# Graph layer on one core: TensorE reads the stored edge messages at register addresses, and VectorE's copies of them go

## The reference

```python
msg = jnp.concatenate([x[row], edge_attr], axis=1)      # row = src, col = dst (sorted)
msg = msg @ W1 + b1                                     # 96 -> 128
agg = jax.ops.segment_sum(msg, col, num_segments=x.shape[0])
out = jnp.concatenate([x, agg], axis=1) @ W2 + b2       # 64 + 128 -> 64
y = layernorm(x + out, axis=-1)
```

## Time and profile before

| | |
|---|---|
| median of three runs | 1054.15 us (1051.51 to 1056.91) |
| profiled execution: first to last instruction (span) | 801.0 us |
| the rest of the median, outside that span | 253.15 us |
| TensorE matmuls busy, share of the span | 615.5 us, 77% |
| TensorE weight loads busy | 544.4 us, 68% |
| VectorE busy | 522.7 us, 65% |
| ScalarE busy | 398.6 us, 50% |
| POOL busy | 423.9 us, 53% |
| mean granted TensorE clock | 0.843 of full speed |

### The profile page before, as it was taken

How to read it: one execution, slowest core, us unless ns; L and a number is a source line. 1 busy time by engine, 2 the same in 40 slices (tenths; PEclk the granted TensorE clock), 3 DMA queues, 4 the chain that set the end, 5 groups by cost and what they waited for, 6 DMA issues and landing times. The chain is left out here.

```text
span 801.0 us, 29016 instructions
## 1 busy us (share of the span) xinstructions
PE 615.5 (77%) x8418; PEld 544.4 (68%) x8419; DVE 522.7 (65%) x1826; ACT 398.6 (50%) x2012; POOL 423.9 (53%) x514
## 2 busy tenths in 40 slices
PE   1345445677778888888898898989898888878785
PEld 1344435566767777777777787878777777768675
DVE  3670111354465648858887788788787787878876
ACT  0011122102234344444567777777777777757655
POOL 5676766711676766475467777767466445200000
PEclk9655555657688779979999999999999999989988
DMA  2121222200223233333345545555455455533432
GB/s 63 28 37 36 37 37 34 57 9 12 61 54 82 59 86 79 79 78 79 100 110 139 127 122 139 129 136 147 115 139 144 110 132 134 134 86 115 126 97 81
DMA packets 168753, 71.47 MB, mean 89 GB/s; under 512 B 61570, under 2 KB 162447, under 8 KB 168720
## 3 DMA queue, kind: packets, MB, share of 16 engines
q1 hardware_dynamic: 104592, 51.74, 22.7%
q0 software_dynamic: 12544, 12.87, 8.5%
q10 hardware_dynamic: 51584, 6.41, 5.1%
HBM read 45.37 MB, written 25.60 MB: 89 GB/s over the span
## 5 line engine op out<-in xcount | busy, mean ns | idle before, releaser
L363 POOL DMA_INDIRECT feat<-in_x,src_now x392 | 393.6, 1004 | 255.4 <-issue 94.6
L775 DVE TENSOR_SCALAR onehot<-node_of_col,group_base,dst_of 128x256 bf16<-128x256 bf16 x952 | 287.4, 348 | 106.1 <-issue 78.9
L473 PEld LDWEIGHTS ps_y<-z_window,onehot 128*128 128x128 bf16 x5712 | 202.6, 101 | 65.8 <-DVE z_window L778 46.0
L473 PE MATMUL ps_y<-z_window,onehot 128*128 128x64 bf16 x5712 | 226.7, 198 | 26.6 <-DVE z_window L778 23.5
L574 ACT ACTIVATE square<-ps_y 128x64 bf16<-128x64 f32 x784 | 162.7, 239 | 135.8 <-PE ps_y L464 133.2
L574 ACT ACTIVATION_READ_ACCUMULATOR square<-ps_y 128x1 f32 x784 | 159.5, 224 | 0.0
L539 ACT ACTIVATE feat_t<-ps_t 97x512 f32<-97x512 f32 x98 | 58.6, 598 | 179.8 <-PE ps_z L400 159.9
L400 PE MATMUL ps_z<-wz,feat_t 97*128 97x64 f32 x784 | 123.1, 324 | 24.6 <-DVE z_rest L700 24.5
L400 PEld LDWEIGHTS ps_z<-wz,feat_t 97*128 97x128 f32 x784 | 118.0, 238 | 33.2 <-DVE z_rest L700 31.8
L392 PE MATMUL ps_t<-ident,feat 128*97 128x128 f32 x392 | 72.3, 333 | 86.8 <-DMA feat<-in_x,src_now 63.7
L464 PE MATMUL ps_y<-wx,x_t 128*128 128x128 f32 x784 | 118.4, 296 | 13.1 <-issue 8.7
(11 more groups left out here) (107 smaller groups left out, 226.2 us busy)
## 6 DMA issues: line engine op xcount, KB each, us to landing
xin<-in_x SPq DMA_DIRECT2D x97, 256.0 KB
out<-yout SPq DMA_DIRECT2D x97, 256.0 KB
feat<-in_x,src_now POOLq DMA_INDIRECT x392
feat<-in_edge_attr ACTq DMA_DIRECT2D x97, 64.0 KB
z<-in_src SPq DMA_DIRECT2D x1, 192.0 KB
z<-in_dst SPq DMA_DIRECT2D x1, 192.0 KB
xin<-in_x SPq DMA_DIRECT2D x1, 128.0 KB
out<-yout SPq DMA_DIRECT2D x1, 128.0 KB
```

Of the source, the lines that this page charges most:

```text
L363: nc.gpsimd.indirect_dma_start(out=feat[h][:, half * CB + c, 0:C], out_offset=None, in_=x[:, :], in_offset=bass.IndirectOffsetOnAxis(ap=sr ...
L473: mm = nc.tensor.matmul(ps_y[h][:, col:col + C], onehot[h][:, g, s, a, :], z_window[h][:, g, s, part * C:(part + 1) * C], start=False, sto ...
L775: ins = nc.vector.tensor_scalar(onehot[h][:, g, s, :, :], node_of_col[:, :, :], base, dst_of[:, bass.ds(firsts[g] + (at + s), 1)], ALU.add ...
```

## The change

VectorE's copy into `z_window` is dropped, with the buffers and the two semaphores that told TensorE of it. `pair_sum` takes its moving operand from `z` itself, at chunk `firsts[g] + at + s`, which is only known in a register. So TensorE reads six numbers of a block's table row (the four firsts as well) before the block, no longer two. Since nothing on VectorE now stands between the last part of `z` and TensorE's reading, TensorE waits for `z_kept` ahead of the units of a round. Two index tables of the set-up that lay in `z_window` get tiles of their own (`chunk_order`). Line numbers after line 120 shift by a few.

```diff
-        z_window = [sb(f"z_window{h}", [P, G, 2, 3 * C], bf16) for h in range(2)]
+        chunk_order = [sb(f"chunk_order{h}", [P, CHUNKS]) for h in range(2)]
...
-                _, (second, third) = load_steps(mybir.EngineType.PE, b, G, 2, G * CHUNKS // 2)
+                _, (*firsts, second, third) = load_steps(mybir.EngineType.PE, b, 0, G + 2, G * CHUNKS // 2)
...
-                def pair_sum(g):
+                def pair_sum(g, at):
...
                                 mm = nc.tensor.matmul(ps_y[h][:, col:col + C], onehot[h][:, g, s, a, :],
-                                                      z_window[h][:, g, s, part * C:(part + 1) * C], start=False, stop=False)
+                                                      z[:, firsts[g] + (at + s), part, :], start=False, stop=False)
...
                 for g in range(G):
-                    pe.wait_ge(window_ready, G * b + g + 1)
                     pe.wait_ge(hot_ready, G * b + g + 1)
-                    pair_sum(g).then_inc(group_summed, 1)
+                    pair_sum(g, 0).then_inc(group_summed, 1)
...
-                        pe.wait_ge(window2_ready, turn_no)
                         pe.wait_ge(hot2_ready, turn_no)
-                        pair_sum(g)
+                        pair_sum(g, 2)
                     with pe.If(third > 0):
-                        _, firsts = load_steps(mybir.EngineType.PE, b, 0, G, CHUNKS - 4)
...
                 edge_round(k)
-                for_units(pe, mybir.EngineType.PE, k - LAG, unit)
+                units_of_round = read_units(mybir.EngineType.PE, k - LAG)
+                pe.wait_ge(z_kept, k - LAG)
+                run_units(pe, *units_of_round, unit)
...
                     ins.then_inc(hot, 1)
-                    nc.vector.tensor_copy(z_window[h][:, g, :, :],
-                                          z[:, bass.ds(firsts[g] + at, 2), :, :].rearrange("p s q c -> p s (q c)")
-                                          ).then_inc(window, 1)
```

More of the change, by code:

```diff
@@ L134, in gnn_residual_layernorm @@
         below, holds = (buf[:, 0:CHUNKS] for buf in x_t)
-        chunk_up, chunk_down = (
-            buf[:, :, :, :].rearrange("p g s q -> p (g s q)").bitcast(f32)[:, 0:CHUNKS] for buf in z_window)
+        chunk_up, chunk_down = (buf[:, :] for buf in chunk_order)
         score, least_row, most_row = (
@@ L179, in gnn_residual_layernorm @@
         hot_ready = sem("onehot_ready")
-        window_ready = sem("z_window_ready")
         group_summed = sem("group_summed")
         hot2_ready = sem("onehot_of_second_pair_ready")
-        window2_ready = sem("z_window_of_second_pair_ready")
         hotx_ready = sem2("onehot_x_ready")
@@ L456, in block_sum @@
                 b = 2 * k + h
-                _, (second, third) = load_steps(mybir.EngineType.PE, b, G, 2, G * CHUNKS // 2)
+                _, (*firsts, second, third) = load_steps(mybir.EngineType.PE, b, 0, G + 2, G * CHUNKS // 2)
+                firsts = [nc.s_assert_within(f, 0, CHUNKS - 4, skip_runtime_bounds_check_because="so the table is made")
+                          for f in firsts]
                 pe.wait_ge(y_kept[h], k + 1)
@@ L525, in _ @@
                 edge_round(k)
-                for_units(pe, mybir.EngineType.PE, k - LAG, unit)
+                units_of_round = read_units(mybir.EngineType.PE, k - LAG)
+                pe.wait_ge(z_kept, k - LAG)
+                run_units(pe, *units_of_round, unit)
             edge_round(PAIRS - 1, loads=2)
+            pe.wait_ge(z_kept, PAIRS - 1 - LAG)
             for_units(pe, mybir.EngineType.PE, PAIRS - 1 - LAG, unit)
@@ L770, in one_hots, with pair @@
                 dve.wait_ge(hots_used[h], k + 1)
-                def pair(g, at, hot, window):
+                def pair(g, at, hot):
                     base = group_base[:, bass.ds(b * G + g, 1)]
@@ L777, in pair @@
                     ins.then_inc(hot, 1)
-                    nc.vector.tensor_copy(z_window[h][:, g, :, :],
-                                          z[:, bass.ds(firsts[g] + at, 2), :, :].rearrange("p s q c -> p s (q c)")
-                                          ).then_inc(window, 1)
                 for g in range(G):
-                    pair(g, 0, hot_ready, window_ready)
+                    pair(g, 0, hot_ready)
                 with dve.If(second > 0):
@@ L786, in one_hots @@
                         dve.wait_ge(group_summed, G * b + g + 1)
-                        pair(g, 2, hot2_ready, window2_ready)
+                        pair(g, 2, hot2_ready)
                     with dve.If(third > 0):
```

## The result

The changed kernel takes 1247.01 us (median of 1244.18, 1247.01 and 1249.96 us) against 1054.15 us: 1.1808 times as long, 95% interval 1.1746 to 1.187, or +193 us. The forecast was 1213 us, +159 us, in a range of 1125 to 1300. The direction and the range held. The gain that it counted on did not come, and part of that miss was cancelled by another.

A forecast was written before the change was run, and what follows sets the result against it. VectorE's loop was taken to set the round, with TensorE close behind. On 1054 us: registers +200, seams +38, table +30, `z_kept` +2, ended waits -101, edge transfers -10, in sum +159, gave 1213 us, range 1125 to 1300.

The forecast's parts named there:

- The register instructions, +200 and +38 us: TensorE's pair sums: twelve register-addressed loads take 0.83 us, not 0.41, +200 us over 476 sums; the seams add +38 us.
- the seams: Between TensorE's pair sums: the next turn's add and first register instruction, 0.08 us x 476 = +38 us.
- The table, +30 us: TensorE's table read before each of 98 blocks: six numbers instead of two, 0 to 60 us, half taken, +30 us.
- The wait for `z_kept`, +2 us: TensorE's new wait ahead of a round's units: already met when reached, one register instruction in 49 rounds, +2 us.
- What goes away, -101 and -10 us: TensorE's waits for copies, `z_rest`, `x_t` and two "issue" gaps end, -101 us; edge transfers come early enough, -10 us.
- the register work hides: Rival: TensorE's register instructions fall beside matmuls, so VectorE's gain comes through, 1002 us; chance 0.04.
- The time outside the span, taken as fixed: The 253.15 us between the profiled span of 801.0 us and the 1054.15 us median, assumed unaffected by the change.
- The clock: Rival: gaps between the sums' matmuls lower TensorE's granted clock, 1268 to 1323, say 1295 us; chance 0.13.
- The condition set: Forecast wrong if rounds lengthen while the granted clock in dense stretches is near 0.75; then the clock is the cause.
- The signs: Profile after: six register instructions per twelve loads over 0.8 to 0.9 us, no line 778, VectorE waiting, rounds 13.5 to 15 us.

The follow-up runs named there:

- without hold-ups: Runs without POOL's indirect gathers, where TensorE's matmuls are not held up: changed kernel 997.17 us, kernel before 764.62 us, fixed chunks 771.36 us.
- The run with idle ones: Fixed chunks and no gathers, plus six register instructions per pair sum that count in a register no matmul uses: 956.15 us, ratio 0.9246.
- fixed chunks: The changed kernel, with pair sums reading z at fixed addresses and no register instructions between their matmuls: 1066.82 us, ratio 1.0104.
- the kernel with the longer read: The kernel before, with TensorE reading six numbers of a block's table row instead of two and using the same two: 1077.97 us, ratio 1.0198.

## Why the prediction was right, and where it was not

**The register instructions, +200 and +38 us: right in kind and in cause, and near in size in the condition they were read from.** 0.42 + 0.08 = 0.50 us a pair sum were forecast; without hold-ups 0.47 were measured (226 us). Of these the sums themselves hold 401.5 - 212.4 = 189 us, 0.40 a pair sum; most of the rest is fp32 work that took longer at a lower clock (160.6 against 122.3 us at the dense products). So the 0.08 us for the seams do not show, the clock takes their place, and that 0.47 comes so close to 0.50 is partly luck. In the timed condition it was 0.38 (180 us): in the first blocks of the rounds the hold-up hides the register work, and in the blocks behind them the lower clock hides part of it. Line 504 of the kernel before was the right place to look.

The prediction had the next load wait for its register instruction. The run with idle ones narrows that: they lengthen four pair sums from 1.56 to 3.02 us, both at full clock, though no load depends on them. The Trainium skill, "TensorE: Matmul & The Clock Gate", section "Architectural detail: the array is 16× 32×32, not 1× 128×128", says that TensorE's queue has 64 entries and that weight loads can be pulled ahead of matmuls in flight. By the same two blocks that does not hide register instructions here.

**The table, +30 us:** 21 us alone (TensorE's reads of six have a median of 1.0 us, not the 1.16 taken from VectorE). **The wait for `z_kept`, +2 us:** no wait of TensorE for the parts of `z` appears in the changed kernel's list.

**What goes away, -101 and -10 us: this is the step that failed.** It said that with VectorE ahead TensorE's waits end and its own sequencer is late next. The missing copies give 10 us in the timed condition, and 0 to 11 us without hold-ups. Two reasons, both shown. In the timed condition VectorE does not set the round, since TensorE is held up about 8 us of it; the waits that the forecast counted were hardly there to be saved. The kernel with gathers of consecutive rows, which has the time and the reads of the kernel before, shows 11.8 us of matmul idle time for the copies, 3.1 for `z_rest` and 5.9 for `x_t`. Without hold-ups the waits moved to the table read and to `x_t`, which lay behind them. Besides, the forecast added up waits of weight loads, 46.0 and 31.8 us; in the same trace the matmuls stood idle only 23.5 us for the copies and 24.5 for `z_rest`, and the rest of those waits passed beside matmuls that were still running. The rival "the register work hides", at 1002 us, rested on the same gain and would have failed by it too.

**The time outside the span, taken as fixed: wrong.** There is none beyond 2 us in any run that has both numbers. The 253 us are hold-ups beside the gathers: the span without gathers is 764.0 us, and with the 39 us that the gathers add ahead of the first unit that makes 803, near the profiled 801. That the hold-ups cost both kernels amounts not far apart (252 and 211 us) made the carrying over from 801 to 1054 us harmless, by luck and not by argument.

**The sum:** 159 - 58 (registers 180 and not 238) - 9 (table) - 2 (`z_kept`) + 101 (copies and transfers 10 and not 111) = +191 us; measured +193. A total within 34 us hides two misses of 58 and 101.

**The clock.** The rival had it as a cause of its own. It is a part of the registers' 180 us: the fp32 groups and the bias matmuls are busy about 37 us longer than with fixed chunks (26 at the dense products, 4 at the bias, 3.5 and 3.1 at the transposes). The condition set, that a clock near 0.75 would make the clock the cause, was badly chosen: 0.72 was granted, but 0.77 with fixed chunks, where the loss is gone.

**The signs.** Six register instructions, 0.82 us a pair sum, no line 778, VectorE waiting several microseconds a round: as told. The doubled busy time of the sums (436.8 against 226.7 us) is a weaker sign than it looks, since 62 us of it stand in the kernel with fixed chunks too (288.9). Rounds of 13.5 to 15 us: only without gathers (15.16); in the timed kernel a median of 21.1, against 19.6 with fixed addresses.

## What to carry to other kernels

A register instruction between small matmuls costs TensorE's stream its own time and more (0.046 us by itself, 189 / 2856 = 0.07 us in the sums and 226 / 2856 = 0.08 us with the clock's share here, beside 1.37 / 48 = 0.03 us for such a matmul), so price a register address by the number of such instructions and let an idle engine copy to a fixed place instead. Before the waits of one engine are booked as a gain, ask what stands behind each of them, by a run with the expensive part taken out. And when a profile's span is far below the timed median, the profile is of another condition: find that first, since here the timed runs held 253 us that the profile did not show, more than the change.

## What the runs showed that was not expected

Indirect gathers that POOL issues freely (one every 1.25 us) slow TensorE's stream to one or two matmuls per 0.75 us for 8 to 9 us a round; the same bytes as plain DMAs do not (765 against 1055 us), and with at most two gathers in flight little of it is left (898 us). With one in flight POOL waited a median of 2.3 us for a landing, and the run's page gives 2.5 us from issue to landing. The Trainium skill, "DMA: Bandwidth & Descriptors", section "Anatomy of one DMA", gives a fixed part of about 2.0 us for a DMA of this path, and the trace is near it.

TensorE is not alone in it. In the kernel with the longer read, register instructions of ScalarE, VectorE and SyncE, which wait for no data, took up to 0.73, 0.72 and 0.72 us. In the profiled execution of the kernel before, without gathers and with plain DMAs none of the three engines had one above 0.17 us. This points to the engines' streams of instructions and not to TensorE's array, though no run tests it. Free issue does not suffice for it: in that profiled execution POOL issued the gathers at nearly the same pace (a median of 1.32 us, against 1.27), and 6 sums had a gap of 0.3 to 1.5 us before them, against 296 in the kernel with the longer read. What the gathers take from the engines, and why that execution was spared, no run here tells.

Without gathers, TensorE's table reads of six numbers leave it idle 0.2 to 1.9 us, mostly ahead of a unit's second block (31.5 us in 50 gaps, 52.6 without the copies), where two numbers left 2.0 us in all.
